# A graph network on one core: three attention stages joined into one, the radial network moved into the last layer

## The reference

```python
# second layer: attention over the edges of a receiver, softmax per receiver
Q, K, V = x @ Wq, x @ Wk, x @ Wv
e = jnp.sum(Q[receiver] * K[sender], axis=-1) * scale
w = jnp.exp(e - segment_max(e, receiver)[receiver])
numer = segment_sum(w[:, None] * V[sender], receiver)
attn = numer / segment_sum(w, receiver)          # 0 where a node has no edge
x = layernorm(x + x + attn @ Wo)

# fourth layer: messages weighted by a small network of the edge length (the radial network)
h = silu(emb @ mlp_w0 + mlp_b0)
h = silu(h @ mlp_w1 + mlp_b1)
w = (h @ mlp_w2 + mlp_b2).reshape(-1, 4, 32)     # four weights per channel and edge
# messages from w, the sender's features and the edge's direction; summed per receiver;
# a matrix on the sums; residual, layer norm
```

## Time and profile before

| what | us |
|---|---|
| median of 3 runs | 5378.56 |
| lowest and highest run | 5373.77 to 5383.27 |
| profiled execution, whole | 5376.34 |
| its span, first to last instruction | 5374.6 |
| busy in the span: POOL | 3855.3 (72%) |
| DVE | 3358.4 (62%) |
| PE | 3172.1 (59%) |
| ACT | 2679.9 (50%) |

### The profile page before, as it was taken

One profiled execution on the slowest core, in us unless ns is written; L12 is line 12 of the kernel. 1 busy time (PEld: TensorE's weight loads), 2 busy tenths in 40 slices (PEclk: granted clock), 3 DMA queues, 4 the chain that ended last, 5 costly groups with the idle time before them and its releaser, 6 DMA issues. The chain is left out here.

```text
span 5374.6 us, 74716 instructions
## 1 busy us (share of the span) xinstructions
PE 3172.1 (59%) x15690; PEld 2478.5 (46%) x15690; DVE 3358.4 (62%) x11850; ACT 2679.9 (50%) x6869; POOL 3855.3 (72%) x3733
## 2 busy tenths in 40 slices
PE   3536555545534664465777465666788866655564
PEld 3536545524323442355666454455455544444442
DVE  6587555568877775575333696333477767666665
ACT  0106666648866886385222375333355554444443
POOL 5777777667766777487777576777677767777777
PEclk9555555579977887798999787888655578888887
DMA  2327777768845775366777786777677643333332
GB/s 73 77 73 225 241 239 238 227 152 250 251 145 160 225 225 180 113 205 194 212 213 214 243 286 206 210 212 212 180 209 208 204 134 101 98 97 98 97 97 74
DMA packets 846208, 953.70 MB, mean 177 GB/s; under 512 B 161164, under 2 KB 570097, under 8 KB 845827
## 3 DMA queue, kind: packets, MB, share of 16 engines
q1 hardware_dynamic: 730304, 765.68, 44.9%
q0 software_dynamic: 112896, 179.36, 14.4%
q10 hardware_dynamic: 2882, 7.36, 0.4%
HBM read 534.20 MB, written 423.34 MB: 178 GB/s over the span
## 5 line engine op out<-in xcount | busy, mean ns | idle before, releaser
L1035 POOL DMA_INDIRECT t_alpha<-gsm_raw,gsm_edge_idx x392 | 386.2, 985 | 165.7 <-issue 118.3
L2110 POOL DMA_INDIRECT mss_xs<-t_x,kept_idx_a x392 | 377.9, 964 | 143.9 <-issue 119.1
L2102 POOL DMA_INDIRECT out_dram<-mss_o,kept_scat_idx x392 | 395.0, 1008 | 119.4 <-issue 117.9
L534 POOL DMA_INDIRECT sort_xd<-in_x_dram,kept_dst_idx x392 | 379.2, 967 | 140.3 <-issue 118.5
L1966 POOL DMA_INDIRECT gs_xs<-t_z,kept_idx_a x392 | 380.5, 971 | 137.5 <-issue 119.2
L1025 POOL DMA_INDIRECT gsm_raw<-t_al,kept_idx_b x392 | 378.2, 965 | 124.1 <-issue 118.9
L1554 POOL DMA_INDIRECT asc_xs<-t_t,kept_idx_a x392 | 370.0, 944 | 134.2 <-issue 110.3
L1856 POOL DMA_INDIRECT gs_xs<-t_t,kept_idx_b x392 | 370.0, 944 | 133.2 <-issue 119.2
L536 POOL DMA_INDIRECT sort_xs<-in_x_dram,kept_src_idx x392 | 379.7, 969 | 119.4 <-issue 118.5
L1227 PE MATMUL gsm_hp<-kept_w,gsm_zT 128*128 128x128 f32 x1568 | 254.9, 311 | 353.5 <-ACT gsm_zT L1093 353.4
L216 PE MATMUL gs_tp<-kept_ident,gs_xs 128*128 128x128 f32 x784 | 271.6, 364 | 250.9 <-DMA gs_xs<-t_t,kept_idx_b 185.1
(11 more groups left out here) (536 smaller groups left out, 11243.8 us busy)
## 6 DMA issues: line engine op xcount, KB each, us to landing
t_t<-sort_o SPq DMA_DIRECT2D x66, 792.0 KB
t_x<-gsm_o SPq DMA_DIRECT2D x196, 264.0 KB
sort_x<-in_x_dram SPq DMA_DIRECT2D x66, 768.0 KB
gsm_x<-t_t SPq DMA_DIRECT2D x196, 256.0 KB
t_z<-gsm_z SPq DMA_DIRECT2D x196, 256.0 KB
out_dram<-gsm_o SPq DMA_DIRECT2D x196, 256.0 KB
t_t<-l_o SPq DMA_DIRECT2D x49, 528.0 KB, 3.1
t_xsrc<-asc_xs SPq DMA_DIRECT2D x98, 264.0 KB, 2.3
```

The lines of the kernel that those rows point to most:

```text
L534: pool.indirect_dma_start(xd[u][:, j, :], None, A["x"], bass.IndirectOffsetOnAxis(K["dst_idx"][:, c:c + 1], 0)).then_inc(gathered[u], 16)
L1035: pool.indirect_dma_start(T["alpha"], bass.IndirectOffsetOnAxis(edge_idx[:, c:c + 1], 0), raw[:, c, :], None).then_inc(scattered[u], 16)
L2102: pool.indirect_dma_start(T["out"], bass.IndirectOffsetOnAxis(K["scat_idx"][:, c:c + 1], 0), o[u][:, j, :], None, bounds_check=N - 1, oob_ ...
L2110: pool.indirect_dma_start(xs[u][:, j, :], None, T["x3"], bass.IndirectOffsetOnAxis(K["idx_a"][:, c:c + 1], 0)).then_inc(gathered[u], 16)
```

## The change

**Attention.** One stage `attention` (att) takes the place of the three. The gathered rows stay in SBUF, in a ring of 16 items; nothing is stored and reloaded, and the two tables `t_xsrc` and `t_radial` are gone. The softmax is made per block of seven items (28 rows of 128 scores), in eight steps on DVE and six on PE, spread over five slots, with the running maximum and sum carried from block to block; a block's earlier sums are faded by one factor where its scan begins. The weights are applied 12 slots behind the scores, by ACT instead of POOL; division and residual are one instruction of DVE (`combine`) instead of a copy on ACT and an addition on POOL. POOL only gathers. The program is written out in full (`in_slots`), without a loop. The scan's flags come as a 64 KB broadcast load per item (`goes`).

**First graph convolution.** It loads `goes` in the same way, and ACT's queue brings `cont` to all partitions in four loads.

**Last layer.** The radial network runs here, item by item; `op` and `up` have one PSUM tile each, to make room for `hp` and `wp`.

```diff
@@ attention: what each engine does in a slot @@
+            in_slots((load, 0, 1, ITEMS), (load_flags, 3, BLOCK, BLOCKS), (load_goes, WEIGHT_LAG - 2, 1, ITEMS),
+                     (load_own, WEIGHT_LAG - 2, 2, PAIRS), (store, WEIGHT_LAG + 7, 2, PAIRS))
...
+            in_slots((turn_weights, FIRST_STEP + 4, BLOCK, BLOCKS), (turn_carried_tops, FIRST_STEP + 2, BLOCK, BLOCKS),
+                     (turn_sums, FIRST_STEP + 3, BLOCK, BLOCKS), (turn_scores, FIRST_STEP + 1, BLOCK, BLOCKS),
+                     (attend, WEIGHT_LAG + 2, 1, ITEMS), (multiply, 1, 1, ITEMS), (turn, 0, 1, ITEMS),
+                     (turn_weighted, WEIGHT_LAG, 1, ITEMS), (turn_tops, FIRST_STEP + 1, BLOCK, BLOCKS),
+                     (turn_carried_sums, FIRST_STEP + 3, BLOCK, BLOCKS))
...
+            in_slots((exponents, FIRST_STEP + 2, BLOCK, BLOCKS), (weight, WEIGHT_LAG, 1, ITEMS), (copy, 0, 1, ITEMS),
+                     (root, WEIGHT_LAG + 4, 2, PAIRS), (apply, WEIGHT_LAG + 5, 2, PAIRS))
...
+            def combine(q):
+                p, half = q // 2, q % 2
+                dve.wait_ge(att_made, q + 1)
+                dve.wait_ge(own_loaded[p % BUFS], 16 * (p // BUFS) + 16)
+                wait_item(dve, applied, p // BUFS, p % BUFS, 4)
+                for j in range(4):
+                    g, c = 4 * half + j, 4 * q + j
+                    st = dve.scalar_tensor_tensor(out=y[p % BUFS][:, g, :], in0=hp[:, j, :], scalar=rdB[:, c:c + 1], in1=own[p % BUFS][:, g, 0:D],
+                                                  op0=ALU.mult, op1=ALU.add)
...
+            in_slots((take_weights, FIRST_STEP + 4, BLOCK, BLOCKS), (scan_tops, FIRST_STEP + 1, BLOCK, BLOCKS),
+                     (shift, FIRST_STEP + 2, BLOCK, BLOCKS), (scan_row_sums, FIRST_STEP + 3, BLOCK, BLOCKS),
+                     (dot, 2, 1, ITEMS), (scan, WEIGHT_LAG + 1, 1, ITEMS), (combine, WEIGHT_LAG + 2, 1, ITEMS),
+                     (measure, WEIGHT_LAG + 3, 2, PAIRS), (scale, WEIGHT_LAG + 4, 2, PAIRS),
+                     (find_flags, FIRST_STEP, BLOCK, BLOCKS), (scan_row_tops, FIRST_STEP + 1, BLOCK, BLOCKS),
+                     (scan_sums, FIRST_STEP + 2, BLOCK, BLOCKS), (invert_sums, FIRST_STEP + 3, BLOCK, BLOCKS))
@@ gcn_first @@
-            pipeline(sp, (load, 0), (load_line, 1), (store, 9))
+            pipeline(sp, (load, 0), (load_goes, 0), (load_line, 1), (store, 9))
...
+            part = EP // 4
+            for k in range(4):
+                act.dma_start(K["cont"][:, k * part:(k + 1) * part], T["cont"][0:1, k * part:(k + 1) * part].broadcast_to([P, part])).then_inc(cont_loaded, 16)
@@ final_edges @@
-        wt = [sb(f"wt{u}", [P, 4, D]) for u in range(BUFS)]
+        wt = [sb(f"wt{v}", [P, 4, D]) for v in range(2)]
...
-        op = [ps(f"op{v}", [P, 4, D]) for v in range(2)]
+        op = ps("op", [P, 4, D])
+        hp, wp = ps("hp", [P, 4, P]), ps("wp", [P, 4, D])
...
-        up = [ps(f"up{v}", [P, 4, D]) for v in range(2)]
+        up = ps("up", [P, 4, D])
...
-                wait_item(pe, msg_ready, t, u, 2)
...
+                wait_item(pe, msg_ready, t, u, 1)
...
-                wait_item(pe, combined, t, u, 2)
...
+                wait_item(pe, combined, t, u, 1)
...
-            pipeline(pe, (turn_x, 1), (turn_back, 9), (project, 3), (reduce, 7), (turn_sums, 5))
+            def radial_first(t, u):
+                wait_item(pe, h2_done, t, u, 1)
+                for pair in range(2):
+                    mm = pe.matmul(hp[:, pair, :], K["m0g"][:, 2 * (u % 2) + pair, :], radial_block(K, t, u), start=True, stop=True)
+                mm.then_inc(h1_ready[u], 1)
...
+            pipeline(pe, (radial_second, 1), (turn_x, 1), (turn_back, 9), (project, 3), (radial_third, 2), (radial_first, 0), (reduce, 7), (turn_sums, 5))
...
-            pipeline(act, (copy_x, 2), (copy_msg, 6), (lambda t, u: norm_root(norm, act, t, u), 11), (scale_x, 0),
+            def radial_one(t, u):
+                act.wait_ge(h1_ready[u], t + 1)
+                act.activation(h1[u % 2][:], hp[:, 0:2, :], ACT.Silu, bias=K["mb0"][:, 0:1]).then_inc(h1_done[u], 1)
...
+            pipeline(act, (radial_two, 1), (copy_x, 2), (radial_one, 0), (copy_msg, 6), (lambda t, u: norm_root(norm, act, t, u), 11), (scale_x, 0),
...
-            pipeline(dve, (scan, 8), (messages, 4), (combine, 10), (lambda t, u: norm_scale(norm, dve, t, u), 11))
+            pipeline(dve, (scan, 8), (messages, 4), (keep, 3), (combine, 10), (lambda t, u: norm_scale(norm, dve, t, u), 11))
```

More of the change, by code:

```diff
@@ L1519, in first_layer, with in_slots @@
     end_stage(nc, owned)
-def attention_scores(nc, A, T, K):
+BLOCK = 7
+BLOCKS = ITEMS // BLOCK
+ROWS = 4 * BLOCK
+RING = 16
+PAIRS = ITEMS // 2
+FIRST_STEP = BLOCK + 1
+WEIGHT_LAG = FIRST_STEP + 4
+assert BLOCKS * BLOCK == ITEMS and PAIRS * 2 == ITEMS
+def in_slots(*parts):
+    for s in range(max(lag + every * (count - 1) for _, lag, every, count in parts) + 1):
+        for f, lag, every, count in parts:
+            if s >= lag and (s - lag) % every == 0 and (s - lag) // every < count:
+                f((s - lag) // every)
@@ L1612, in _, with multiply @@
[L1612 to L1616 removed]
+                    tr = pe.transpose(tp[:, j, :], xd[q % BUFS][:, j, :], K["ident"][:])
+                tr.then_inc(turned, 1)
+            def multiply(q):
+                pe.wait_ge(copied, q + 1)
+                if q >= 2:
+                    pe.wait_ge(dotted, q - 1)
+                for j in range(4):
+                    mm = pe.matmul(qp[q % 2][:, j, :], xdT[q % 2][:, j, :], K["wqk"][:], start=True, stop=True)
+                mm.then_inc(multiplied, 1)
@@ L1792, in apply, with exponents, root @@
+            def exponents(b):
+                act.wait_ge(soft_v, V_STEPS * b + 4)
+                act.activation(e[:], shifted[:], ACT.Exp).then_inc(exped, 1)
+            def root(p):
+                norm_root(norm, act, p // BUFS, p % BUFS)
+            def apply(p):
+                t, u = p // BUFS, p % BUFS
                 act.wait_ge(norm["scale_ready"][u], t + 1)
@@ new lines, in shift @@
+            def shift(b):
+                dve.wait_ge(soft_p, P_STEPS * b + 3)
+                dve.wait_ge(soft_v, V_STEPS * b + 3)
+                link(dve.tensor_copy(carried[:, 0:2], small[0:ROWS, 0:2]))
+                dve.scalar_tensor_tensor(out=ahead[:], in0=unjoined[:, 0, :], scalar=carried[:, 0:1], in1=ahead[:], op0=ALU.add, op1=ALU.max)
+                link(dve.scalar_tensor_tensor(out=back[:], in0=unjoined[:, 1, :], scalar=carried[:, 1:2], in1=back[:], op0=ALU.add, op1=ALU.max))
+                link(dve.tensor_tensor(top[:], ahead[:], back[:], ALU.max))
+                dve.tensor_tensor(shifted[:, 0:P], scores[:], top[:], ALU.subtract)
+                dve.tensor_scalar(shifted[0:1, P:P + 1], top_ahead[:, 0:1], top[0:1, 0:1], 0.0, ALU.subtract, ALU.min).then_inc(soft_v, 1)
@@ new lines, in scan @@
+            def scan(q):
+                dve.wait_ge(weight_turned, q + 1)
+                dve.wait_ge(goes_loaded[q % BUFS], 16 * (q // BUFS) + 16)
+                if q >= BUFS:
+                    dve.wait_ge(att_made, q - BUFS + 1)
+                if q >= 1:
+                    dve.wait_ge(scanned, q)
+                first = sc[(q - 1) % BUFS][:, 4 * P - 1:4 * P]
+                if q and q % BLOCK == 0:
+                    link(dve.tensor_tensor(start[:], first, fade[q // BLOCK % 2][:], ALU.mult))
+                    first = start[:]
+                dve.tensor_tensor_scan(sc[q % BUFS][:], goes[q % BUFS][:], wtp[q % 2][:].rearrange("p j i -> p (j i)"), first,
+                                       ALU.mult, ALU.add).then_inc(scanned, 1)
```

507 lines of the change are left out of this document (243 added, 264 removed).

## The result

The changed kernel takes **5628.06 us** (median of 4 runs, 5625.01 to 5634.66), the kernel before 5378.3 beside it: a ratio of 1.0466, 95% interval 1.0448 to 1.0484, slower. The forecast was 5576 with a range of 5450 to 5720. The profiled execution took 5625.35 us, its span is 5623.7.

What follows compares the result with a forecast made beforehand. POOL bounds the last stage and scores before; afterwards a loop through DVE, PE and ACT bounds the last stage and DVE attention. 5376.3 + 301 (last stage) - 106 (attention) + 5 (first graph stage) = 5576 us, range 5450 to 5720.

Steps and rivals of the forecast that it cites:

- Attention, -106 forecast: Attention merged into one stage: DVE becomes the bound, 725 us against 830.7, bounds 665 to 790.
- the trips: Attention: four times a block DVE waits at the front of a slot for PE, 2.8 us a block.
- The turn, 13.36 forecast: Last stage: one pass of the loop through three engines takes one slot, 13.36 us against POOL's 10.3; bounds 12.5 to 14.5.
- forecast loop: Last stage: DVE's scan to `combine`, PE's `turn_back` to `radial_first`, ACT's Silu to root, DVE's `norm_scale`; 13.36 us.
- the second Silu and its table load on ACT (1.31 + 0.47) lie beside DVE's 5.59 and are free: Last stage: this ACT work was taken to add nothing to the 13.36 us turn.
- PE's `turn_back` waits for DVE's `y`: Last stage: one of the signs that were to show the loop, with scans 13 us apart.
- Head and tail, 160 forecast: Last stage outside the 87 whole turns: 75 us ahead of them and 85 behind.
- The faster case: Rival, last stage: loop costs less than the merge gives, turn under 11.1 us; 5275 us if under POOL's 10.3; chance 0.06.
- The lower clock: Rival, last stage: PE's clock level falls, radial matmuls double (+1.8), `project` +0.5 a turn; 5776 us; chance 0.06.
- A switch of tables that costs twice the row: Rival, last stage: the root waits for an engine drain, a switch takes twice 1.31 us; 5690 us; chance 0.04.
- The rival in which attention gains nothing: Attention: DVE's hand-offs to PE and ACT cost 8 us more a block, 830 instead of 725; 5680 us; chance 0.08.
- The first graph stage: Added broadcast load per item and four `cont` loads, mostly hidden by POOL's gathers: 0 to 35 us, taken as +5.

Runs made afterwards that it cites:

- e5: Changed kernel with only `turn_x` moved on PE in the last stage, to the end of the slot: 5627.99 us.
- e3: Changed kernel with only `turn_back` moved on PE in the last stage, behind `reduce`: 5608.68 us.
- e1: Changed kernel with PE's last-stage order rewritten: `radial_first` and `reduce` right behind `turn_x`, `turn_back` next to last: 5284.76 us, 0.9822 of the kernel before.
- e6: Changed kernel with `turn_back` and `turn_x` both moved on PE in the last stage, behind `reduce` and `turn_sums`: 5506.39 us.
- after: The changed kernel itself, without further edits: 5628.06 us, 1.0466 of the kernel before.

## Why the prediction was right, and where it was not

- **Attention, -106 forecast, -107.6 measured.** Right in its bound (DVE). That the sum came out within 2 us is in part luck, for its terms were off and cancel: additions 1.10 for 0.95 (98 x 0.15 = 15 us more) and the root's waits 36 and more for 10 (26 more), against dots 1.14 for 1.31 (98 x 0.17 = 17 less), the trips 2.1 us a block for 2.8 (10 less) and a pair's statistics and scale 2.65 + 0.52 for 3.33 (49 x 0.16 = 8 less). The last 8 us were not traced. The 1.249 us a gather that the prediction gives for the scores was worked out from the row of the first graph stage; the scores' own row gives the same, (2979.1 - 2490.8) / 391.
- **The turn, 13.36 forecast, 13.65 measured** ((5524.59 - 4350.46) / 86, first to last of the 87 reciprocals that wait for the root). Each link of the forecast loop is within 0.2 us of its row, PE's being the one that grew most (4.41 for 4.22), and in one turn of four DVE's scan starts 0.55 us late with no wait that the profile names. e5, where this loop stands alone, has the same turn, 13.66. So this part was right in its mechanism and mis-sized by 0.29: 87 x 0.29 = 25 of the 49 us by which the last stage was over.
- **The step that failed: "the second Silu and its table load on ACT (1.31 + 0.47) lie beside DVE's 5.59 and are free".** They lie beside it, but on a path of their own. From the root, ACT's `scale_x`, `apply`, load and `radial_two` take 4928.22 - 4923.52 = 4.70 up to the start of `copy_x`, and `copy_x`, its hand-off and `turn_x` another 1.65 up to `turn_back`, 6.35 in all; DVE's way from the root to the end of `combine` takes 6.21. So the forecast's sign "PE's `turn_back` waits for DVE's `y`" came out as 6.8 us in 1100, and a cure made by the forecast (e3) gains 0.3% where it would have promised 3.5%. The time came out because the forecast loop alone gives it (e5) and the other is of the same length to some 0.15 us; that the loop left out is no longer than that is luck.
- **Head and tail, 160 forecast, 184 measured:** the first root's reciprocal, at 4350.46, stands at the end of the first turn, so 4350.46 - 13.65 - 4252.1 = 84.7 lie ahead of the turns for 75, and 5623.7 - 5524.59 = 99.1 behind them for 85. These 24 us are the other half of the 49. The slots ahead were priced at 5 to 7 us up to the first root; scans 8 to 12 come 10.2, 8.5, 11.8 and 13.3 us apart already, as scan, `combine` and root join in one after the other. The slots behind still run at 10.4 to 12.5 while messages last (DVE's scans 5525.00, 5536.46, 5548.95, 5559.38).
- **The rivals.** The faster case needed a turn of 11.1; it was 13.65. POOL-bound, as that rival had it, is what e1 gives, 5284.76 for the 5275 named. The lower clock is in the trace, yet not as that rival put it: in the turn shown it covers `turn_x` to `project` and mostly spares the radial matmuls, which cost 4920.77 - 4918.94 = 1.83 to the next Silu for 1.81 forecast. A switch of tables that costs twice the row didn't come: the copy ends at 4922.21, the load starts at 4922.23, the root at 4923.52, so 1.31 in all. The Trainium skill (ScalarE: Activation LUTs, "What ACT_TABLE_LOAD costs") counts 2.66 with its drain. The trace doesn't agree: the 88 loads ahead of the root have 1.6 us of idle time before them in all. The rival in which attention gains nothing fell with its first row, 723.1 us for 830.7.
- **The first graph stage** came to +7.4 (3728.9 - 3214.0 = 514.9, 507.5 before) for +5.

## What to carry to other kernels

Where engines take the steps of a slot in fixed orders, list every step that waits for another engine in its own slot, and follow each back to itself: a loop that closes within one slot sets the beat with the sum of all its links, however idle each engine looks (here 13.65 us with none of them over 62% busy). When one loop is found, look for the next before pricing a cure, since cutting one of two loops of equal length gains little or nothing (31 of the 350 us in e3, none in e5), and behind both there can be a third (the tie by `up` in e6); only the order of e1, which opens all of them, gave back nearly all of the 350. In an order written by hand, steps that nobody in the same slot waits for go last, and those that feed another engine go first: that one line made the changed kernel 6.1% faster.

## What the runs showed that was not expected

PE's granted clock differs here between turns and within a turn, and with it the length of a loop. Behind waits of about 5 us the four matmuls of `radial_third` took 1.35 us in the turn shown of after, with `turn_x`, `turn_back` and `project` ahead of them, and 1.91 in eleven turns of twelve of e3, without `turn_back`. A cure that moves a wait, or what runs first behind it, can so give a part of its gain back: the turn of e3 came to 13.37 us on average where 12.65 was due, and one of 12.32 shows what the higher level would give. And two cures for waits on one engine can give more together than apart (63.4 for 49.5 us in attention), when each alone uncovers the other's wait.
